# Attention inside one kernel: probabilities transposed by VectorE and carried by DMA instead of transposed by TensorE

## What is computed

```python
xn = layernorm(x)                                  # [1, 1024, 512]
qkv = xn @ w_qkv.T                                 # 32 query heads, 8 key/value heads, head size 128
scores = einsum('bskgd,btkd->bkgst', qh, kh) / sqrt(128)
scores = where(tril, scores, finfo.min)            # causal
probs = softmax(scores, -1)
attn = einsum('bkgst,btkd->bskgd', probs, vh)
s = attn @ w_dense.T                               # back to width 512
h = relu(s0 * xn @ W0) * 2                         # W0, W1, W2: 512x512 matrices of +1 and -1
h = relu(s1 * ei(h) @ W1) * 2                      # ei: the last fifth of the columns times -4
g = silu(s2 * ei(h) @ W2)
out = x + s * g
```

## Time and profile before

| | before |
|---|---|
| median of three runs | 1057.82 us |
| profiled execution: span from first to last instruction | 1053.9 us |
| median run minus this span | 3.9 us |
| TensorE busy | 1037.8 us, 98% |
| VectorE busy | 669.0 us, 63% |
| ScalarE busy | 520.0 us, 49% |
| GpSimd busy | 340.6 us, 32% |
| mean granted TensorE clock | 0.997 |

### The profile page before, as it was taken

One profiled execution on the slowest core, in us unless ns is written; L12 is line 12 of the kernel. 1 busy time (PEld: TensorE's weight loads), 2 busy tenths in 40 slices (PEclk: granted clock), 3 DMA queues, 4 the chain that ended last, 5 costly groups with the idle time before them and its releaser, 6 DMA issues.

```text
span 1053.9 us, 17118 instructions
## 1 busy us (share of the span) xinstructions
PE 1037.8 (98%) x5424; PEld 882.4 (84%) x5424; DVE 669.0 (63%) x1454; ACT 520.0 (49%) x1077; POOL 340.6 (32%) x298
## 2 busy tenths in 40 slices
PE   6999999999999999999999999999999999999998
PEld 5888888888888888888888888888888888888886
DVE  8576557756586566765577565865567555666543
ACT  3564446544475445644465444753456444545442
POOL 5242324323143222322143321432323231434533
PEclk9999999999999999999999999999999999999999
DMA  5120001100020001100021000210012000000021
GB/s 189 32 61 11 1 1 51 49 0 0 0 70 30 0 0 33 57 10 0 0 60 40 0 0 0 70 30 0 0 40 56 4 0 0 21 11 1 1 91 60
DMA packets 17015, 28.35 MB, mean 27 GB/s; under 512 B 2144, under 2 KB 3680, under 8 KB 16992
## 3 DMA queue, kind: packets, MB, share of 16 engines
q1 hardware_dynamic: 16992, 28.06, 8.7%
HBM read 25.95 MB, written 2.10 MB: 27 GB/s over the span
## 4 chain that ended last, share of the span: by engine, by line
PE 97%; DVE 2%; DMA 0%; ACT 0%; SPq 0%; issue 0%; ACTq 0%; DVEq 0%
PE ps_m L963 14%; PE ps_m L965 14%; PE ps_m L964 14%; PE ps_t L1013 12%; PE ps_o L965 6%; PE ps_o L963 6%; PE ps_s L965 6%; PE ps_s L964 6%; PE ps_o L964 6%; PE ps_s L963 6%; PE ps_m L1105 3%; PE ps_s L1089 1%; PE ps_m L1061 1%; DVE half_var L784 0%; DMA prob_odd<-x 0%; DVE prob_odd L833 0%
## 5 line engine op out<-in xcount | busy, mean ns | idle before, releaser
L644 POOL TENSOR_TENSOR prob_even<-prob_even,row_inv 128x128 f32<-128x128 f32 (+3 forms) x128 | 135.5, 1070 | 389.5 <-DVE row_inv L819 389.5
L644 POOL TENSOR_TENSOR prob_odd<-prob_odd,row_inv 128x256 f32<-128x256 f32 (+3 forms) x128 | 162.8, 1283 | 276.8 <-DVE row_inv L819 276.8
L716 ACT ACTIVATE pt_hi<-ps_t 128x512 fp32r<-128x512 f32 x288 | 171.3, 598 | 157.9 <-PE ps_t L1013 155.8
L878 DVE TENSOR_TENSOR pt_lo<-ps_t,pt_hi 128x512 fp32r<-128x512 f32 x288 | 197.1, 687 | 72.7 <-ACT pt_hi L716 71.7
L810 DVE CUSTOM_DVE_ANT_0 ps_s<-ps_s,mask 128x128 f32<-128x128 f32 (+7 forms) x256 | 192.9, 766 | 40.5 <-PE ps_s L965 39.8
L963 PE MATMUL ps_m<-xn_hi,w_hi 128*128 128x512 f32 (+1 forms) x376 | 150.4, 400 | 1.3 <-DVE xn_lo L870 0.7
L965 PE MATMUL ps_m<-xn_hi,w_lo 128*128 128x512 f32 (+1 forms) x376 | 147.1, 391 | 0.0
L964 PE MATMUL ps_m<-xn_lo,w_hi 128*128 128x512 f32 (+1 forms) x376 | 147.0, 391 | 0.0
L686 ACT ACTIVATE prob_odd<-ps_s,neg_max 128x256 f32<-128x256 f32 (+3 forms) x128 | 101.6, 795 | 87.9 <-DVE neg_max L810 87.5
L963 PE MATMUL ps_s<-k_hi,q_hi 128*128 128x512 f32 (+5 forms) x384 | 138.8, 361 | 0.0
L965 PE MATMUL ps_s<-k_hi,q_lo 128*128 128x512 f32 (+5 forms) x384 | 131.1, 341 | 0.0
(11 more groups left out here) (108 smaller groups left out, 1598.5 us busy)
## 6 DMA issues: line engine op xcount, KB each, us to landing
raw<-wqkv SPq DMA_DIRECT2D x48, 256.0 KB, 2.6
raw<-wd SPq DMA_DIRECT2D x32, 256.0 KB, 2.6
prob_odd<-x SPq DMA_DIRECT2D x8, 256.0 KB, 4.1
out<-y SPq DMA_DIRECT2D x8, 256.0 KB, 2.0
prob_even<-x SPq DMA_DIRECT2D x7, 256.0 KB, 4.3
raw<-k SPq DMA_DIRECT2D x3, 256.0 KB, 2.8
raw<-x SPq DMA_DIRECT2D x1, 256.0 KB, 2.5
scales<-s SPq DMA_DIRECT2D x3, 0.5 KB, 3.2
```

Of the source, the lines that this page charges most:

```text
L644: pool.tensor_tensor(rows, rows, row_inv[:, slot:slot + 1] .to_broadcast([P, (i + 1) * P]), ALU.mult)\
L716: act.activation(pt_hi[:, t % PT_RING, :, :], ps_t[t % TURN_RING][:, :, :], ACT.Copy).then_inc(turn_hi, 1)
L878: dve.tensor_tensor(pt_lo[:, t % PT_RING, :, :], ps_t[t % TURN_RING][:, :, :], pt_hi[:, t % PT_RING, :, :], ALU.subtract)\
```

## The change

The transposes leave TensorE. What stands in their place, for each row of a group:

1. The softmax tile is no longer one head by 128 queries but four heads by 32 queries (`tile` r = 0 to 3, partition = head*32 + query). `q_hi` and `q_lo` are laid out so that such a tile is one stationary operand. Tile r of row i needs (4i+r+1)*32 keys rather than (i+1)*128. Each tile's maximum reads one contiguous stretch of `ps_s`.
2. "norm" of tiles 0 to 2 goes to ScalarE, tile 3 stays on GpSimd.
3. "flip": VectorE transposes the whole row of probabilities, 128 x (i+1)*512 elements, in place in 32x32 blocks, one instruction for each row.
4. "move": SP issues 16 SBUF-to-SBUF DMAs for each row (4 query tiles x 4 heads); each carries 32 partitions x (i+1) runs of 128 floats into `pt_lo`, which has 12 slots. Rows share slots, so some moves wait until older blocks have been weighed (`LAND_AFTER`).
5. "land": ScalarE writes `pt_hi` from `pt_lo`, GpSimd subtracts it from `pt_lo` in place; "weigh" then reads both.
6. The exp of row i waits for the landing of row i-2.
7. GpSimd takes over VectorE's low parts of the weights (`split`). The banks of `ps_t` go to a second `ps_o` and a second `ps_m`, so two evictions can be under way.
8. Row 0 of the next group is scored, moved and landed inside the body before (its number is 8 there); for group 0 the prologue does it.
9. In the last part, x is fetched back for the residual after all landings of the even rows, and the fourth silu buffer lies in `prob_odd`.

The order lists are planned anew with other costs and leads. The core of the diff:

```diff
+Q = 32
+TILES = P // Q
...
-TURN_RING = 2
-PT_RING = 4
+HI_RING = 4
+LAND = 12
...
+NORMS_ACT = 3
+MOVES = TILES * HEADS
...
+LAND_AT = [0, 1, 3, 6, 1, 6, 0, 4]
+COLUMNS = [list(range(i + 1)) for i in range(BLOCKS)]
+COLUMNS[6].reverse()
+
+LAND_AFTER = {0: tri(7), 2: 30 - PAIRS, 3: 34 - PAIRS, 4: tri(3), 5: tri(4), 6: tri(5) + 1, 7: tri(6) + 3}
...
+def width(i, r):
+
+    return (i * TILES + r + 1) * Q
+
+
+def score_banks(i, r):
+
+    return [r] if i < 4 else [2 * (r % 2), 2 * (r % 2) + 1]
+
+
+def score_parts(i, r):
+
+    w = width(i, r)
+    if i < 4:
+        return [(r, 0, w, 0)]
+    a = (w // Q + 1) // 2 * Q
+    return [(2 * (r % 2), E - a, a, 0), (2 * (r % 2) + 1, 0, w - a, a)]
...
+            task("dve", ("max", i, r), 0.32 + w / 960, ("scores", i, r))
+            task("act", ("exp", i, r), 0.45 + w / 1185, ("max", i, r), ("landed", i - 2))
+            task("dve", ("inverse", i, r), 0.16, ("exp", i, r))
+            if r < NORMS_ACT:
+                task("act", ("norm", i, r), 0.3 + w / 1200, ("inverse", i, r))
+            else:
+                task("pool", ("norm", i, r), 0.2 + w / 600, ("inverse", i, r))
+        task("dve", ("flip", i), 0.1 + (i % BLOCKS + 1) * 0.535, *[("norm", i, r) for r in range(TILES)])
+        after = LAND_AFTER.get(i % BLOCKS, 0)
+        task("sp", ("move", i), 0.47 * MOVES, ("flip", i),
+             *([("weigh", *pairs[after - 1])] if after > 0 else []))
+        for j in COLUMNS[i % BLOCKS]:
+            t = pair_no(i, j) if i < BLOCKS else PAIRS
+            task("act", ("hi", ("land", i, j)), 0.63, ("landed", i),
+                 *([("weigh", *pairs[t - HI_RING])] if t >= HI_RING else []))
+            task("pool", ("lo", ("land", i, j)), 1.29, ("hi", ("land", i, j)))
...
+    for r in tiles:
+        act += [("exp", first, r)]
...
+    act += hi(*values) + [("norm", first, r) for r in tiles if r < NORMS_ACT] + hi(("land", first, 0))
...
+    dve += lo(*values) + [("flip", first)]
...
+        def prob_rows(i):
+
+            size = prob_size[i % 2]
+            return probs[i % 2][:, size - (i % BLOCKS + 1) * E:size]
+
+        def prob_tile(i, r):
+
+            tiles = prob_rows(i).rearrange("p (u c) -> p u c", c=P)
+            return tiles[:, 0:width(i % BLOCKS, r) // Q, r * Q:(r + 1) * Q]
...
-        ps_t = [ps(f"ps_t{n}", [P, HEADS, P]) for n in range(TURN_RING)]
-        ps_o = ps("ps_o", [P, HEADS * P])
-        ps_m = ps("ps_m", [P, E])
+        ps_o = [ps(f"ps_o{n}", [P, HEADS * P]) for n in range(2)]
+        ps_m = [ps(f"ps_m{n}", [P, E]) for n in range(2)]
...
+                    elif what == "move":
+                        i, = item
+                        row = i % BLOCKS
+                        sp.wait_ge(flipped, r.row_no(i))
+                        sp.sem_inc(flips_seen)
+                        if kind != "prologue" and row in LAND_AFTER:
+
+                            sp.wait_ge(block_weighed, WEIGHED0 + PAIRS * g + LAND_AFTER[row])
+                        tiles = prob_rows(i).rearrange("p (j b c) -> p j b c", b=TILES, c=P)
+                        slots = slice(LAND_AT[row], LAND_AT[row] + row + 1)
+                        for b in range(TILES):
+                            for h in range(HEADS):
+                                sp.dma_start(pt_lo[b * Q:(b + 1) * Q, slots, h * P:(h + 1) * P].bitcast(F32),
+                                             tiles[h * Q:(h + 1) * Q, :, b, :])\
+                                  .then_inc(landed[i % 2], 16)
...
-                        pool.tensor_tensor(rows, rows, row_inv[:, slot:slot + 1]
-                                           .to_broadcast([P, (i + 1) * P]), ALU.mult)\
-                            .then_inc(normed, 1)
+                        i, tile = item
+                        slot = (TILES * i + tile) % STAT_RING
+                        rows = prob_tile(i, tile)
+                        pool.wait_ge(inverse_done, r.score_no(i, tile))
+                        pool.tensor_tensor(rows, rows, row_inv[:, slot:slot + 1, None].to_broadcast(
+                            [P, width(i % BLOCKS, tile) // Q, Q]), ALU.mult).then_inc(normed_pool, 1)
+                    elif what == "lo" and item[0][0] == "land":
+                        _, i, j = item[0]
+                        t = r.pair(i, j)
+                        slot = LAND_AT[i % BLOCKS] + j
+                        hi_slot = 0 if i == BLOCKS else pair_no(i, j) % HI_RING
+                        pool.wait_ge(land_hi, t)
+                        pool.tensor_tensor(pt_lo[:, slot, :], pt_lo[:, slot, :].bitcast(F32),
+                                           pt_hi[:, hi_slot, :], ALU.subtract).then_inc(land_lo, 1)
...
+                        if tile == 0 and kind != "prologue":
+
+                            act.wait_ge(landed[i % 2], LANDED0[i % 2] + r.landings(i - 2))
+                        act.wait_ge(max_done, r.score_no(i, tile))
+                        act.activation(prob_tile(i, tile), as_tiles(score_row(i, tile)),
                                        ACT.Exp, scale=-1.0, bias=neg_max[:, slot:slot + 1],
                                        accum_out=row_sum[:, slot:slot + 1]).then_inc(exp_done, 1)
+                        continue
+                    if what == "norm":
+                        i, tile = item
+                        slot = (TILES * i + tile) % STAT_RING
+                        rows = prob_tile(i, tile)
+                        act.wait_ge(inverse_done, r.score_no(i, tile))
+                        act.activation(rows, rows, ACT.Copy, scale=row_inv[:, slot:slot + 1])\
+                            .then_inc(normed_act, 1)
...
-                        act.activation(pt_hi[:, t % PT_RING, :, :], ps_t[t % TURN_RING][:, :, :],
-                                       ACT.Copy).then_inc(turn_hi, 1)
+                        t = r.pair(i, j)
+                        hi_slot = 0 if i == BLOCKS else pair_no(i, j) % HI_RING
+                        if j == COLUMNS[i % BLOCKS][0]:
+                            act.wait_ge(landed[i % 2], LANDED0[i % 2] + r.landings(i))
+                        act.wait_ge(block_weighed, WEIGHED0 + t - HI_RING)
+                        act.activation(pt_hi[:, hi_slot, :],
+                                       pt_lo[:, LAND_AT[i % BLOCKS] + j, :].bitcast(F32),
+                                       ACT.Copy).then_inc(land_hi, 1)
...
+                    if what == "flip":
+                        i, = item
+                        dve.wait_ge(normed_act, NORMS_ACT * r.row_no(i))
+                        if NORMS_ACT < TILES:
+                            dve.wait_ge(normed_pool, (TILES - NORMS_ACT) * r.row_no(i))
+                        dve.transpose(prob_rows(i), prob_rows(i)).then_inc(flipped, 1)
...
-                    elif name == "turn":
-                        _, i, j = item
-                        t = tri(i) + j
-                        dve.wait_ge(turn_hi, TURNS * g + t + 1)
-                        dve.tensor_tensor(pt_lo[:, t % PT_RING, :, :], ps_t[t % TURN_RING][:, :, :],
-                                          pt_hi[:, t % PT_RING, :, :], ALU.subtract)\
-                            .then_inc(turn_split, 1)
...
-                    elif name == "split":
-                        piece = item[1]
-                        slot = r.raw_slot(piece)
-                        dve.wait_ge(w_hi_done, r.piece_no(piece))
-                        if piece.startswith("wd"):
-                            hi, lo = (w[:, int(piece[2]), :] for w in (wd_hi, wd_lo))
-                        else:
-                            hi, lo = (w[:, PIECES.index(piece), :, :].rearrange("p c d -> p (c d)")
-                                      for w in (w_hi, w_lo))
-                        dve.tensor_tensor(lo, raw[:, slot, :], hi, ALU.subtract).then_inc(w_split, 1)
...
+                        q_tile = [q[:, q0, :, :].rearrange("p h s -> p (h s)") for q in (q_hi, q_lo)]
+                        for score_bank, first, n, k0 in score_parts(row, tile):
+                            mm = three(banks4[:, score_bank, first:first + n],
+                                       q_tile,
+                                       (k_hi[:, k0:k0 + n], k_lo[:, k0:k0 + n]), True, True)
...
-                    elif name == "turn":
-                        _, i, j = item
-                        t = tri(i) + j
-                        pe.wait_ge(turn_split, TURNS * g + t + 1)
-                        if j == 0:
-                            pe.wait_ge(normed, SCORES * g + HEADS * (i + 1))
-                        for h in range(HEADS):
-                            mm = pe.transpose(ps_t[t % TURN_RING][:, h, :],
-                                              probs[i % 2][:, h, j * P:(j + 1) * P], ident[:, :])
-                        mm.then_inc(turned, 1)
                     elif name == "weigh":
                         _, i, j = item
-                        t = tri(i) + j
                         if (i, j) == (0, 0):
```

(14 more changed lines are left out.)

639 lines of the change are left out of this document (323 added, 316 removed).

## The result

The changed kernel took 1081.78 us, the median of 4 runs (1071.42 to 1082.39), against 1057.41 for the kernel before (4 runs, 1056.32 to 1058.14). The ratio of the runs is 1.0213, with a 95% interval of 1.0171 to 1.0256: slower by 2.1%. Forecast were 944 us and a range of 920 to 1008; the profiled execution has a span of 1080.7 us, 140 us over the 940.4 of the sum.

The account below looks back on a forecast made before the run. TensorE bound the kernel before; afterwards its 105.3 us and a row path of 103 were both near, giving 107 a body. Sum: 41.4 + 11 + 7 x 107 + 139 + 3.9 = 944 us, range 920 to 1008.

Parts of the forecast that it names:

- the price of an issue: SP's time to issue one move, taken from four loads: 0.453 us, bounds 0.35 to 0.60; 62.5 us a body.
- Rival 2: DMA packets in the moves are dear: even with before at 68 ns, 1141 us at 86 ns; chance 0.07.
- the packet: DMA time for 512 bytes in the moves: 27 ns taken, range 27 to 86.
- 103 us of path: Chain of exps, norm, flip, move and landing through a body's rows: 87 us without queues plus 16 for queues.
- 105.3 of TensorE: TensorE's floor for a body: 122.6 us less 17.3 for transposes and narrower scores.
- SP was taken: In the path without other queues, row 2's landing came at 21.2 us because SP was occupied.
- 4 us a row for all queues together: Waiting on ScalarE, GpSimd and VectorE in each of four odd rows: some 4 us, 16 a body.
- Rival 5: TensorE idles in every body until its clock drops: some 5 us more per body, 980 us; chance 0.06.
- The first body: ScalarE waits for row 0's landing, TensorE idles 6 to 8 us, then runs at half clock: 11 us more.
- TensorE's saving: Per group, 15.8 us from transposes removed and scores from 25.5 to 24.0 us: together 17.3 us.
- rival 3: SP's moves don't overlap, each taking 2.6 us in turn: 333 us per group, over 2700 us; chance 0.01.
- rival 1: The row path sets the body through costlier queues or brittle order: 110 to 120 us, total 999; chance 0.25.

Follow-up runs that it names:

- Experiments 7 and 8: Changed kernel with four wide, unpermuted moves in rows of one parity, sixteen in the others: odd rows at four 1006.05 us, even rows at four 1038.55 us.

## Why the prediction was wrong

**The step that failed is the price of an issue.** The sum took 0.453 us from four loads and gave it bounds of 0.35 to 0.60, for "the three-dimensional patterns". The measured 0.65 lies outside. The doubt was put on the shape, and the shape made no difference (0.46 us for the move's own shape read from memory); what sets the dear issues apart is SBUF at both ends, which no row of before has. Rival 2 came near, with "no row shows SBUF as source", and then looked for the price in the packet. It is not quite so: the eight stores of before have SBUF as source, at 0.34 us, and they would not have warned.

**What hangs on it.** A move takes 10.4 us for the 7.25 of the sum, landed 12.3 us after the first issue for 9.4. The prediction let 103 us of path stand beside 105.3 of TensorE and took 107. In the terms of the spans, with the move of row 1 in the first and the last turn as marks (65.87 and 937.92 us), of which the sum made 56.9 and 805.9:

| part | forecast | measured | more |
|---|---|---|---|
| up to row 1's move, first body | 56.9 (41.4 + 11 + 4.5) | 65.9 | 9.0 |
| seven bodies | 749.0 | 872.1 | 123.1 |
| from row 1's move in the last turn | 134.5 | 142.8 | 8.3 |

The 17.5 us that a body has over 107 divide, by the runs, into 2.2 that were not due to the moves' number (109.2 with four issues a row) and 15.3 that went with it. The wide moves' packets are also faster (28.5 against 34.5 ns), and they land together and not one by one, so 109.2 is not exactly the body of a kernel with cheap narrow issues; no run could give SP that.

**SP is a queue in the path, not a load beside it.** The prediction had SP at 60% and concluded that it was no bound. It is at (83 + 5) / 124.5 = 71% and is still no bound by load; but each of the 16 issues lies wholly within the path of its row, and the other parity's 10.3 us can stand in front. The prediction noted that once ("SP was taken") and put 4 us a row for all queues together. Experiments 7 and 8 price it: the even rows' issues, which that sum had off the path except in row 2, are 5.6 us of each body. The loads that share the queue were put at nothing; in the body shown row 1's flip is over at 440.3 us and its moves start at 441.34, behind a load that waited for GpSimd, so they cost about 1 us. The Trainium skill ("Perfetto Trace Analysis", What "DMA-bound" means) calls a kernel bound by its DMA sequencer where that track is solid with DMAs. SP's track is at 71% here, so by that rule this kernel isn't, and yet the one with a quarter of the issues is 126 us faster: the rule does not catch issues that lie in a chain.

**The softmax stage was sized too small.** From row 3's last landing to row 5's flip the sum had 1.0 us + 0.837 ns x 2880 columns for the exps and 1.6 for the last inverse and norm: 5 us. It took 15.1. The landing is seen on ScalarE's timeline (start us, duration, idle before it and its releaser), with row 5's first exp behind four high parts of row 3:

```profile
476.00 2.20 ACT L830 ACTIVATE pt_hi<-pt_lo 128x512 fp32r<-128x512 f32 x4 [0.38 <-DMA pt_lo<-prob_odd]
478.11 0.80 ACT L786 ACTIVATE prob_odd<-ps_s,neg_max 128x672 f32<-128x672 f32 x1
```

TensorE, same columns, the scores of row 5's third tile:

```profile
481.43 0.33 PE L1066 MATMUL ps_s<-k_hi,q_hi 128*128 128x384 f32 x1
```

VectorE, same columns, up to the flip:

```profile
487.02 1.00 DVE L924 CUSTOM_DVE_ANT_0 ps_s<-ps_s,mask 128x800 f32<-128x800 f32 x1 [1.42 <-PE ps_s L1068]
487.94 0.16 DVE L933 RECIPROCAL row_inv<-row_sum 128x1 f32<-128x1 f32 x1
489.52 1.03 DVE L924 CUSTOM_DVE_ANT_0 ps_s<-ps_s,mask 128x832 f32<-128x832 f32 x1 [1.43 <-PE ps_s L1068]
490.47 0.69 DVE L1031 TENSOR_TENSOR y<-ps_m,y 128x512 f32<-128x512 f32 x1
491.07 3.37 DVE L941 STREAM_TRANSPOSE prob_odd<-prob_odd 128x3072 f32<-128x3072 f32 x1
```

The inverse of row 5's last tile (487.94) stands behind row 6's first maximum (800 columns), which waits for its scores; the flip stands behind row 6's second maximum and an eviction. The third tile's scores need the banks of the first, whose exp is over at 479.0; TensorE comes to them only at 481.43, because its list has projections and a weigh in front. So 4 us were set for the queues of a row, and row 5 needed 10. This is a second term that was too small, beside the price of an issue. With four moves a row the same queues leave a body of 109.2 us, near the 107; that they only count where the moves leave the path no room is my reading, and no run takes them away alone.

**The clock.** TensorE's mean granted clock is 0.955, 0.997 before. One steady body of the changed kernel as a stretch (busy us (count) of PE, PEld, DVE, ACT, POOL, clock, DMA share, GB/s):

```profile
425.40:549.50 124.10, 111.00 (x501) 90.19 (x500) 65.62 (x135) 74.14 (x154) 66.90 (x55) 0.97 0.40 97
```

and one of the kernel with four moves:

```profile
362.80:472.10 109.30, 106.61 (x502) 88.49 (x501) 65.05 (x135) 73.99 (x155) 67.09 (x55) 1.00 0.38 110
```

The same matmuls take 4.4 us more. In this stretch TensorE fell to its lower level (0.50, 1.2 GHz) twice, just after it had been idle for 3.6 and for 2.2 us:

```profile
468.00:470.00 2.00, 2.00 (x7) 1.94 (x8) 0.75 (x2) 1.71 (x4) 1.95 (x2) 0.50 0.42 98
...
544.00:546.00 2.00, 2.00 (x5) 1.43 (x6) 0.00 (x0) 0.98 (x2) 2.00 (x2) 0.50 0.11 26
```

Rival 5 had this mechanism, 5 us a body, but for a kernel at 107. How much of the 4.4 us lies on the path no run tells; it is a consequence of the waits and goes with them.

**The first body** was forecast 11 us longer, and TensorE to idle 6 to 8 us. It idles 12.6: its next scores need a bank that an exp of row 1 frees, and ScalarE is at those exps only when row 0 has landed (timeline of TensorE: start us, duration, idle before it and its releaser):

```profile
45.05 0.40 PE L1068 MATMUL ps_m<-xn_hi,w_lo 128*128 128x512 f32 x1
58.03 0.61 PE L1066 MATMUL ps_s<-k_hi,q_hi 128*128 128x288 f32 x1 [12.58 <-ACT prob_odd L786]
58.43 0.44 PE L1067 MATMUL ps_s<-k_lo,q_hi 128*128 128x288 f32 x1
```

The mechanism was right, the lower clock behind the gap too (granted clock 0.53 from 58 to 62 us; 0.44 us for a matmul of 288 columns against 0.28 for one of 256 in the earlier trace rows); the work in front was over 2.5 us sooner than I had it, and the move 3 us longer.

**What was right.** TensorE's saving: no transposes, 4272 matmuls for 5424, and 912 us busy in the kernel with four moves against 1037.8, 126 less where the sum said 8 x 17.3 = 138. The flips: 4.436 us for 4096 elements and 1.239 for 1024 were forecast as 4.38 and 1.23. The landings on GpSimd, 1.295 us, and on ScalarE, 0.623. The packet was off, and it cost nothing: those of 512 bytes took 34.5 ns on average in the trace, between the 27 of the sum and the 38 that the prediction estimated from the Trainium skill ("SBUF — State Buffer", Door 1: The DMA port swizzle). At 34.5 row 7's 256 packets an engine need 8.8 us, under the 10.6 that SP takes for its issues. Rival 2, in which dear packets make the kernel slower, needed 68 ns and is out; so is rival 3, moves that don't overlap. (Rival 3 calls most of the moves smaller than 64 KB; those of three rows in eight are.) The outcome is rival 1's, the row path sets the body, with 124.5 us where it was given 110 to 120: its own price was computed with the same 0.453.

**Chances.** Rival 1 had 0.25 and slower 0.07. The two limits 103 and 105.3 were known to be close, so every microsecond on the path would count four to eight times a body; the range should have put the path's one unmeasured price, 128 times in a body, at the far ends of what DMA could cost, and not 23 to 32% around the row of another kind. At 0.65 the method of the prediction itself gives 4 x 3 us more path and, with SP's queue, some 115 to 120 us a body: 41.4 + 14 + 7 x 115 (120) + 141 + 3.9, 1005 to 1040 us. So the price of an issue, put right, gives 61 to 96 of the 138 us that were missing; the other 42 to 77 lie in what the method still has too small, the queues at 4 us a row above all; no run divides them further.

## What to carry to other kernels

Price a DMA issue by both of its ends as well as by the number, and count it on the path, not as a share of its queue: 16 issues of 0.65 us in front of a result are 10 us of latency, whether each carries 16 or 128 KB. Where a change takes work off the busiest engine and puts a chain in its place, write down the chain's length against the engine's, and treat each price in it that no row shows as the first thing to measure. If a chain that recurs in each turn can't be shortened, start its first link a turn earlier: here that, with new order lists, was worth 72 us, and turned 2.1% slower into 4.4% faster.

## What the runs showed of the hardware

- A DMA from SBUF to SBUF of 32 to 256 runs over 32 or 64 partitions takes 0.62 to 0.66 us of its queue's time in the kernel that only issues and in the narrow moves, whether a run has 512 bytes or 2 KB; with 16 bytes it was 0.63 behind the wide moves of row 1. A DMA of 128 runs of 2 KB from memory takes 0.45 to 0.52, one of 128 runs of 512 bytes 0.46. A store from SBUF to memory takes 0.34 alone, 0.46 each for the first four in a row and 0.65 for the next four. A load of 512 runs from memory took 0.61 (seven in 4.29 us), so the number of runs or the data behind them does count there.
- Large moves slow the issue of the next: over 128 partitions 0.67 us at 256 KB, 0.90 at 384, 1.04 at 512 (four in a row); over 64 partitions 1.24 at 256 KB (eight in a row).
- A packet of 512 bytes from SBUF to SBUF took 34.5 ns on average over 32 partitions, 36.1 over 64 and 28.5 over 128; the loads of before took 27.1.
- SP's and ScalarE's queues issue side by side, 0.74 and 0.70 us each where one alone takes 0.65.
- VectorE turns 32x32 blocks of f32, 128 partitions, at 1.04 ns per element and partition over 0.17 us, as fast as it reads them for a maximum.
